# Attention of sixteen heads: the element work on a batch's two halves, four operations against two

## What is computed

```
x = x + _L0_attn_a_ref(_layernorm(x), ...)     # two convolutions, 4 linear attentions, a feed-forward
x = x + _L0_ffn_ref(_layernorm(x), ...)        # 8 experts, the best one
x = x + _L0_attn_b_ref(_layernorm(x), ...)     # attention, stage a0
x = x + _L0_ffn_ref(_layernorm(x), ...)
x = x + _L1_attn_a_ref(_layernorm(x), ...)     # causal attention, stage a1
x = x + _L1_ffn_ref(_layernorm(x), ...)        # 8 experts, the best two
x = x + _L1_attn_b_ref(_layernorm(x), ...)     # attention, stage a2
x = x + _L1_ffn_ref(_layernorm(x), ...)
```

```
qkv = x @ Wqkv + bqkv
q, k, v = jnp.split(qkv, 3, axis=-1)               # each to (B, 16, T, 8)
scores = jnp.einsum('bhtd,bhsd->bhts', q, k) * scale
scores = jnp.where(causal[None, None], scores, -jnp.inf)
weights = jax.nn.softmax(scores, axis=-1)
y = jnp.einsum('bhts,bhsd->bhtd', weights, v)
return y @ Wo + bo
# a0: q and k are RMS-normalised, no bias, no mask; afterwards y = y - sum(y * Vn) * Vn with Vn = v / |v|
# a2: q and k are RMS-normalised with weights, bias, no mask, no scale
```

## Time and profile before

| what | value |
|---|---|
| device time, median of 3 executions | 2546.61 us (2541.16 to 2558.46) |
| device time of the profiled execution | 2553.93 us |
| its span, first to last instruction | 2552.2 us |
| busy in the span: PE, DVE, ACT, POOL | 1951.2, 1462.8, 1140.9, 1132.5 us |
| mean granted clock of PE, as a share of 2.4 GHz | 0.854 |

### The profile page before, as it was taken

How to read it: one execution, slowest core, us unless ns; L and a number is a source line. 1 busy time by engine, 2 the same in 40 slices (tenths; PEclk the granted TensorE clock), 3 DMA queues, 4 the chain that set the end, 5 groups by cost and what they waited for, 6 DMA issues and landing times. The chain is left out here.

```text
span 2552.2 us, 44162 instructions
## 1 busy us (share of the span) xinstructions
PE 1951.2 (76%) x14950; PEld 1367.1 (54%) x14950; DVE 1462.8 (57%) x4272; ACT 1140.9 (45%) x2591; POOL 1132.5 (44%) x1973
## 2 busy tenths in 40 slices
PE   7969999987847887867888877794278888485991
PEld 6858888875423333434555456674034443264871
DVE  6978888845745554866667623222277676232232
ACT  3434555543427775433555543342056654351440
POOL 2424555532445553464565653143635444324134
PEclk9989999998868998977899979897577777687996
DMA  7000000000000000000000025373000000044572
GB/s 241 1 1 1 1 1 1 1 1 1 0 0 1 1 2 1 1 0 1 2 2 2 18 88 156 118 208 107 12 1 1 2 1 12 23 137 124 151 211 82
DMA packets 93938, 109.44 MB, mean 43 GB/s; under 512 B 12944, under 2 KB 76832, under 8 KB 93600
## 3 DMA queue, kind: packets, MB, share of 16 engines
q1 hardware_dynamic: 85536, 89.96, 12.0%
q0 software_dynamic: 8192, 16.79, 2.3%
HBM read 78.14 MB, written 28.57 MB: 42 GB/s over the span
## 5 line engine op out<-in xcount | busy, mean ns | idle before, releaser
L1493 DVE TENSOR_REDUCE a2mx<-PS 128x4 f32<-128x1024 f32 x128 | 156.0, 1218 | 97.0 <-PE PS L1680 66.2
L1935 ACT ACTIVATE a2prob<-PS 128x512 f32<-128x512 f32 x256 | 144.9, 600 | 108.5 <-PE PS L1704 91.7
L1493 DVE TENSOR_REDUCE a1mx<-PS 128x6 f32<-128x768 f32 x128 | 122.1, 954 | 75.8 <-PE PS L1687 74.3
L1938 ACT ACTIVATE a0prob<-PS 128x1024 f32<-128x1024 f32 x128 | 127.3, 1028 | 50.4 <-PE PS L1704 50.0
L1935 ACT ACTIVATE a1prob<-PS 128x384 f32<-128x384 f32 x256 | 114.1, 496 | 77.2 <-PE PS L1704 76.4
L278 PE MATMUL PS<-cv_rT,cv_diag 128*128 128x256 f32 x640 | 143.1, 383 | 0.0
L239 DVE SCALAR_TENSOR_TENSOR cv_y<-cv_gl,k_conv_w,cv_y 128x256 f32<-128x256 f32 x320 | 131.3, 477 | 18.8 <-ACT cv_y L347 11.0
L1328 POOL TENSOR_SCALAR_AFFINE_SELECT a1prob<-a1prob 128x256 f32<-128x256 f32 x256 | 97.2, 408 | 98.9 <-ACT a1prob L1935 97.8
L2419 DVE TENSOR_SCALAR m1bhid<-PS,m1bwr 128x256 f32<-128x256 f32 x92 | 40.3, 480 | 169.9 <-PE PS L2510 97.2
L2419 DVE TENSOR_SCALAR m1ahid<-PS,m1awr 128x256 f32<-128x256 f32 x92 | 40.3, 479 | 165.5 <-PE PS L2510 88.1
L278 PEld LDWEIGHTS PS<-cv_rT,cv_diag 128*128 128x128 f32 x640 | 121.9, 192 | 17.1
(11 more groups left out here) (535 smaller groups left out, 5517.2 us busy)
## 6 DMA issues: line engine op xcount, KB each, us to landing
m1awr<-in_wtab SPq DMA_DIRECT2D x46, 514.0 KB
m1bwr<-in_wtab SPq DMA_DIRECT2D x46, 514.0 KB
rows_in<-cv_blank SPq DMA_DIRECT2D x46, 128.0 KB, 2.1
m1axin<-rows_in SPq DMA_DIRECT2D x46, 128.0 KB
rows_out<-m1ayo SPq DMA_DIRECT2D x46, 128.0 KB
m1bxin<-rows_in SPq DMA_DIRECT2D x46, 128.0 KB
rows_out<-m1byo SPq DMA_DIRECT2D x46, 128.0 KB
X<-in_x SPq DMA_DIRECT2D x4, 512.0 KB, 6.5
```

What stands on the lines that cost most here:

```text
L1493: v.tensor_reduce(mx[:, 2 * j:2 * j + 2, :], MB[:, :, 0:SEG * seg_len].rearrange("p h (s n) -> p h s n", n=seg_len), AX.X, ALU.max).then_i ...
L1935: act.activation(prob[:, h % RING, 0:n_prob], SB[(b * NH + h) % NSB][:, 0:n_prob], ACT.Exp, scale=scale).then_inc(s["exp"], 1)
L1938: act.activation(prob[:, h % RING:h % RING + EXPS, :], PS[:, h % NSB:h % NSB + EXPS, :], ACT.Exp, scale=scale).then_inc(s["exp"], EXPS)
```

## The change

Where DVE took the two halves of a batch with one operation each, it takes both with one.

- The raw step (only with the maximum): it waits for `qkv1` and `qkv0` first and then takes both halves of q and k (128x512) and both of v (128x256) in one operation each. So that the two banks lie in order in memory, half 0 now goes to M0 and half 1 to M1. PE multiplies half 1 first (M1 is free first), waits for `qh1`, then half 0. `prepare_rT` accordingly waits for `qkv0`.
- The casts (all three stages): one operation of 128x512 for q and one for k.
- `complete_y` (all three stages): one reciprocal of 128x32 and one product of 128x256.

```
-            bank_qkv, bank_k, bank_q = (M1, M0), M1, M0
+            bank_qkv, bank_k, bank_q = (M0, M1), M1, M0
...
+                if keep_max:
+                    v.wait_ge(s["qkv1"], b + 1)
+                    v.wait_ge(s["qkv0"], b + 1)
+                    for dst, lo, hi in ((heads(qk[:, :, :]), 0, 2 * C), (va[:, b % 4, :, :, 0:HD], 2 * C, 3 * C)):
+                        add = g[name + "_bqkv"][:, lo:hi].rearrange("p (n d) -> p n d", d=HD)
+                        last = v.tensor_tensor(dst, heads(PS[:, 6:8, lo:hi]),
+                                               add.unsqueeze(1).broadcast_to([P, NT, (hi - lo) // HD, HD]), ALU.add)
+                    last.then_inc(s["raw"], 1)
+                    return
...
-                    for t in range(NT):
-                        src = qk[:, t, w * C:(w + 1) * C].rearrange("p (n d) -> p n d", d=HD)
-                        last = v.tensor_copy(rows[:, t, :, 0:2 + w:1 + w], src.unsqueeze(2).broadcast_to([P, NH, 2, HD]))
+                    src = heads(qk[:, :, w * C:(w + 1) * C])
+                    last = v.tensor_copy(rows[:, :, :, 0:2 + w:1 + w], src.unsqueeze(3).broadcast_to([P, NT, NH, 2, HD]))
...
-                cols = [(M0, M1)[h][:, :].rearrange("p (n r) -> p n r", r=RW) for h in range(NT)]
-                for h in range(NT):
-                    last = v.reciprocal(den[:, h, :], cols[h][:, :, HD])
-                last.then_inc(s["den"], 1)
+                cols = PS[:, 6:8, :] if keep_max else PS[:, 5:7, :]
+                cols = cols.rearrange("p t (n r) -> p t n r", r=RW)
+                v.reciprocal(den[:, :, :], cols[:, :, :, HD]).then_inc(s["den"], 1)
                 v.wait_ge(s["den"], b + 1)
-                for h in range(NT):
-                    last = v.tensor_tensor(y[:, h, :].rearrange("p (n d) -> p n d", d=HD), cols[h][:, :, 0:HD],
-                                           spread(den[:, h, :], HD), ALU.mult)
-                last.then_inc(s["y"], 1)
+                v.tensor_tensor(heads(y[:, :, :]), cols[:, :, :, 0:HD],
+                                den[:, :, :].unsqueeze(3).broadcast_to([P, NT, NH, HD]), ALU.mult).then_inc(s["y"], 1)
...
+                        prepare_qkv(b + AHEAD1, 1)
+                        pe.wait_ge(s["qh1"], b + 1)
                         prepare_qkv(b + AHEAD1, 0)
-                        pe.wait_ge(s["qh1"], b + 1)
-                        prepare_qkv(b + AHEAD1, 1)
...
-                finished(act, s["qkv1"], b - 1)
+                finished(act, s["qkv0" if keep_max else "qkv1"], b - 1)
```

More of the change, by code:

```diff
@@ L1860, in _ @@
             if keep_max:
+                prepare_qkv(0, 1)
                 prepare_qkv(0, 0)
-                prepare_qkv(0, 1)
                 pe.wait_ge(s["raw"], 1)
                 prepare_rt(1)
+                prepare_qkv(1, 1)
                 prepare_qkv(1, 0)
-                prepare_qkv(1, 1)
                 pe.wait_ge(s["raw"], 2)
@@ L1872, in _ @@
                 pe.wait_ge(s["kT"], 1)
+                prepare_qkv(2, 1)
                 prepare_qkv(2, 0)
-                prepare_qkv(2, 1)
                 for j in range(PAIRS):
```

## The result

| | kernel before | changed kernel |
|---|---|---|
| device time, median of 15 executions each, us | 2552.27 (2541.16 to 2561.91) | 2569.2 (2558.11 to 2574.25) |
| ratio, with its 95% interval | | 1.0061 (1.0045 to 1.0077) |
| device time and span of the profiled execution, us | 2553.93, 2552.2 | 2558.11, 2556.4 |
| busy PE, DVE, ACT, POOL, us | 1951.2, 1462.8, 1140.9, 1132.5 | 1955.5, 1444.1, 1143.5, 1137.2 |

The change makes the kernel 0.6% slower, about 16 us; the forecast was 0.2% faster. The profiled execution of the changed kernel is its fastest, so the pair of profiles differs by 4 us and the medians by 17. I take from the profiles where a stage changed, and from the timed runs how much.

What follows compares the result with a forecast made beforehand. It took PE's fixed order of steps, idling where it waits for DVE, to bound the attention stages. Terms a0 -4.9, a1 -1.6 and a2 +2.3 sum to -4.2 us: 2542 us from the 2546.6 median, range 2516 to 2568.

Steps and rivals of the forecast that it cites:

- raw step in a1: a1: merged raw step 0.13 us shorter where lo comes last; in 4 batches about 0.4 us later, +1.6 us.
- a0's -4.9: a0: the chain from y to qkv's second half gets 0.35 us shorter a batch, 14 batches: -4.9 us.
- the 0.14 of the casts: Casts: two merged ones take 0.76 us where four took 0.90, saving 0.14 us a batch.
- y's -1.0: a1: y comes 0.08 us earlier and PE waits for it, 12 batches: -1.0 us.
- Unit costs: DVE's merged operations: two casts 0.76 us, raw step 1.02, y's product 0.42; reciprocal saves about 0.01.
- The term costed at nothing: a0: POOL must stand aside for one longer cast, 0.42 us in place of 0.28; costed at 0, at most 0.14 a batch.
- the chain: a1: casts, POOL's lo, raw step, ot; ot 0.27 us earlier in 8 of 13 batches, -2.2 us.
- the step that failed: a2: merged raw step ends 0.40 us later in 9 of 13 batches, delaying ot: +3.2 us, stage sum +2.3.
- rival C: PE's clock: shifted waits move batches between slow and fast kinds; slow 2564 us, chance 0.10; fast 2518, chance 0.15.
- The forecast named the mark for it: Sign of the clock rival: a2 shorter or longer than 442 us by over 5 with the same waits.
- A: a1 and a2: DVE waits for the later matmul in all 26 batches, +9.4 us, 2556 us; chance 0.13.
- B: Merged casts lose their fast rate, two taking 1.30 us: +2 us, 2549 us; chance 0.07.

Runs made afterwards that it cites:

- e2: Kernel before with only the casts and complete_y merged, in all three stages: ratio 0.9961 (0.9940 to 0.9981), 2544.9 us against 2558.1.
- e3: Changed kernel with the raw step merged only in a1, not in a2: 0.9931 of the kernel before, 2542.1 us against 2558.1.
- e4: Changed kernel with the raw step merged only in a2, not in a1: 1.0066 of the kernel before, 2574.5 us against 2558.1.
- e6: Kernel before, nothing merged, but in a2 DVE waits for both halves before its four operations: ratio 1.0125, 2579.9 us against 2549.9.
- e7: Kernel before, with two useless fills by DVE ahead of the raw step's signal in a2: ratio 1.0110, 2575.2 us against 2549.9.
- g1: Changed kernel measured again in another job: 1.0040 (1.0019 to 1.0061) of the kernel before, 2565.0 us against 2554.3.
- g2: Changed kernel with four unread matmuls ahead of PE's wait for the raw step in a2: 0.9944 of the kernel before, 2543.5 us against 2554.3.
- e5: Changed kernel with PE taking the ot step one head later in a2: 0.9991 of the kernel before, 2546.2 us against 2549.9.
- e1: Kernel before with only the raw step merged, in a1 and a2: ratio 1.0090 (1.0071 to 1.0110), 2582.0 us against 2558.1.
- e8: Kernel before with only the casts merged, in all three stages: ratio 0.9976 (0.9957 to 0.9994), 2543.3 us against 2549.9.
- e12: Kernel before with only complete_y merged, in all three stages: ratio 0.9961 (0.9932 to 0.9990), 2430.5 us against 2440.7.
- e9: Changed kernel with four unread matmuls ahead of PE's raw-step wait in a2: 0.9933 of the kernel before, 2422.8 us against 2440.7.
- e10: Kernel before with four unread matmuls ahead of PE's raw-step wait in a2: ratio 0.9973 (0.9948 to 0.9998), 2436.0 us against 2440.7.

## Why the prediction was wrong

The time of 2542 us was wrong, and in sign; 2569 us lies 1 us outside the range. By parts, forecast against measured (ratios times the kernel before's 2552 us):

| part | forecast, us | measured, us |
|---|---|---|
| casts and y, all stages | -7.4 | -10 (-15 to -5), e2 |
| raw step in a1 | +0.5 | about 0 to -8, e3 and e4 |
| raw step in a2 | +2.7 | +27 (some 19 to 34), e4 against e2 |

(The forecast's parts are its own terms sorted anew: a0's -4.9, the 0.14 of the casts in 8 batches of a1 and 3 of a2, y's -1.0; the rest is the raw step's.)

- **Unit costs: right.** 0.42 us a cast, 0.76 the pair; 0.60 from the raw step's first start to its second and 0.41 for that one; reciprocal 0.35; y 0.42.
- **a0: right in sign and place.** Forecast 0.35 a batch, measured 0.24 at the place and 0.2 in the step from ot to ot (15.0 to 14.8). The term costed at nothing, POOL's product beside the longer cast, was 0.11, within the bound of 0.14 given for it. PE's wait between the halves of qkv went from 16.8 to 14.0 us, not towards 12, and its next wait, for POOL's part of y, rose from 18.6 to 22.8 over the stage: it is now 1.4 us in each of the first twelve batches, before in eight of them. The stage went down by 6.5 us all the same, more than the steps explain, with the clock from 0.87 to 0.90; the expert stage behind it, which the forecast took to be untouched, gave 3 to 6 us back.
- **a1: the chain right, its yield too small.** In the usual batch PE's wait went from 1.48 to 1.22 us as forecast, and every step of the two usual kinds is 0.3 shorter, at most 4 us over the loop; the rest of the profile's 10 us came with a clock of 0.88 in place of 0.84, and the kernels with the same a1 that took 358 us show that it doesn't come with the edit every time. The sums of the waits did not fall: ahead of ot 14.7 us in 11 where the earlier trace rows has 14.5, and for y 10.1 in 12 where it has 9.7 in 11; y's 0.08 can't be seen in them. (Waits of PE, 1200 to 1480 us.)

```profile
PE PS L79 <- DVE a1va L1459: 14.7, 11, 2.5
...
PE PS L79 <- DVE a1y L1526: 10.1, 12, 1.2
```

- **a2: the step that failed.** "In 7 ot now starts within 0.1 us of the raw step's end and in 2 it has 0.2 us of slack: 7 x 0.40 + 2 x 0.20 = +3.2". Batch by batch the delay is there: from qkv's end to ot 1.21 us in place of 0.72, and a wait in 12 of 13 batches. As waiting it comes to little, since some long waits went: 4.3 us in 12 against 3.8 in 7 before. But the sum took the delay for the whole cost and set the clock beside it, as rival C with a chance of its own. It is not independent: in this place the same delay, by a merge (e4), a wait (e6) or two fills (e7), brings PE's clock down, and the clock costs several times the delay. The forecast named the mark for it (a2 off by over 5 us with the same waits) and the size, +22 on the sum, 2564. It had a chance of 0.10 and is what came.
- **The short wait and the clock.** The clock went from 0.77 to 0.71 with the merge and its wait, and from 0.70 to 0.77 with the filler in the wait. The forecast left open whether so short a wait matters: in this place it does, 21.5 us (g1 to g2). e5 bounds it: waits as long at the next step went with 0.82. The Trainium skill ("TensorE: Matmul & The Clock Gate", Part 1) has it that activity releases the clock and idling takes it back. The filler agrees with it (0.70 to 0.77). The sum of PE's idle time in the stretch does not: it is 29 to 35 us in the six kernels that lose time in a2 (changed, g1, e1, e4, e6, e7; clock 0.67 to 0.73) and 31 to 42 in the twelve others (0.77 to 0.82).
- **In what currency.** The forecast added up waits, and waits are not what moved the stages. PE's idle time went, before to after, (windows as shown) from 72.5 to 73.2 us in a0, from 75.1 to 79.5 in a1 and from 34.4 to 35.0 in a2's stretch; its busy time, for as many matmuls, by -7.7, -14.9 and +17.5.
- **A and B fell.** a1 did not turn to the join (its usual steps got shorter), and no cast lost its rate.
- **Open.** How the clock decides: the sum of the short waits is no measure of it (e5; e3 has 4.3 us of them ahead of ot in five batches and a clock of 0.80, e7 2.0 in nine and 0.73). What these six kernels share is a wait ahead of ot in each batch but the last of the stretch; that it is this which counts was not tested. That the delay acts through the clock is shown by the filler, for a2 alone; why a0 and a1 gained in clock was only argued, from shorter waits. Why the second expert stage runs at the lower clock for longer once a0 is shorter was not tried. Casts alone (e8) have a0 at 276.0 and y alone (e12) at 277.4, both together at 271.2: that they don't add there is only seen, not explained.

## What to carry to other kernels

Where the clock stands between its levels (0.77 here), a wait of PE can cost more than its length, as it did in a2: look in the windows at how PE's busy time for the same matmuls differs, and price a new wait by what the clock would do, before the delay itself. Merging two operations on halves saves their fixed part (0.07 us here) and takes away the overlap with the producer of the second half: do it where another input comes last (POOL's lo in a1), not where the producer does (a2). If a delay has to stay, give it cover (a step of other work, e5), or fill it with matmuls that nobody reads (g2).

## What was not expected

The job of e9 to e12 ran the kernel before in 2440.7 us in place of some 2555. What was absent there are stalls around POOL's indirect transfers of the expert stages. Waits in the kernel before's first profile that have no releaser in the program, or a DMA (total, times, longest; DVE, then ACT):

```profile
DVE m1bhid L2419 <- remote: 48.1, 3, 33.3
DVE a2mx L1493 <- DMA m1agy<-rows_out,m1apos: 30.2, 3, 16.8
```

```profile
ACT a2yT L1951 <- remote: 23.3, 1, 23.3
```

The step of a2 during which POOL issues its scatters one behind the other took 56.4 us there, 56.5 in the changed kernel, and 17.7 to 18.0 in e9, e10 and e12: 38 of the 110 us. None of the edits touches it. What sets it was not tried; each of the last four jobs ran on another chip, so the chip is one candidate.
